# A wait for landing behind every group of four gathers on GpSimd

## The reference

```
q = (h @ Wq.T + bq)[dst];  k = (h @ Wk.T + bk)[src];  v = (h @ Wv.T + bv)[src]
alpha = sum(q * k, -1) / 4
ex = exp(alpha - segment_max(alpha, dst)[dst])
out = segment_sum(ex / segment_sum(ex, dst)[dst] * v, dst)
```

```
msg = silu([x[src], x[dst], rbf(length)] @ mw1 + mb1) @ mw2 + mb2
agg = segment_sum(msg, dst) / count
```

## Times and profile before

| | us |
|---|---|
| median of three timed runs | 5630.9 |
| the profiled execution, its span | 7840.1 |
| PE busy in it | 4625.7 (59%) |
| DVE busy | 4037.4 (51%) |
| POOL busy | 3849.3 (49%) |
| ACT busy | 2769.9 (35%) |
| share of the DMA engines' time, queue of the gathers | 23.6% |

### The profile page before, as it was taken

The page is one execution under the profiler, slowest core; times in us unless marked ns, Lnnn a source line. Parts: engine busy times, 40 slices in busy tenths (PEclk is TensorE's granted clock), DMA queues, the critical chain, the costliest instruction groups (busy, mean ns, idle before and its releaser), DMA issues.

```text
span 7840.1 us, 106032 instructions
## 1 busy us (share of the span) xinstructions
PE 4625.7 (59%) x22831; PEld 3727.9 (48%) x22832; DVE 4037.4 (51%) x11107; ACT 2769.9 (35%) x6493; POOL 3849.3 (49%) x4066
## 2 busy tenths in 40 slices
PE   4555555655556556555555565555555656666667
PEld 2444444534444445344444453444444545555555
DVE  4555555645555556455555565555555553333334
ACT  1333333423333334233333342333333432323333
POOL 3555555335555553345555543455555425555553
PEclk6666666676666666766666667666666677877887
DMA  5222222222322222222223222222322211111111
GB/s 127 78 79 76 77 76 78 52 66 73 79 78 77 78 80 56 69 67 79 76 78 79 78 62 69 68 78 77 80 78 79 60 33 43 44 44 44 44 44 30
DMA packets 267188, 536.13 MB, mean 68 GB/s; under 512 B 116253, under 2 KB 148689, under 8 KB 266509
## 3 DMA queue, kind: packets, MB, share of 16 engines
q0 software_dynamic: 180992, 490.24, 23.6%
q1 hardware_dynamic: 78901, 35.89, 1.9%
q10 hardware_dynamic: 6936, 6.69, 0.3%
HBM read 512.41 MB, written 18.03 MB: 68 GB/s over the span
## 4 chain that ended last, share of the span: by engine, by line
PE 26%; another core or an unknown queue 26%; issue 20%; DVE 17%; ACT 5%; DVEq 4%; ACTq 1%; SPq 0%; DMA 0%; POOL 0%; POOLq 0%
PE bank L806 9%; PE bank L825 7%; DVE acc L1265 6%; ACT oh L556 2%; DVEq L333 2%; PE bank L797 2%; PE bank L851 2%; PE bank L810 1%; DVE alpha L1288 1%; PE bank L879 1%; DVEq L1265 1%; DVE slots L1361 1%; DVE oh L1249 1%; PE bank L1001 1%
## 5 line engine op out<-in xcount | busy, mean ns | idle before, releaser
L508 POOL DMA_INDIRECT slots<-kv_table,idx x3224 | 3065.2, 951 | 3133.0 <-PE bank L825 1275.8
L825 PE MATMUL bank<-slots,oh 128*128 128x136 f32 (+1 forms) x8060 | 1593.0, 351 | 569.1 <-DVE acc L1265 506.4
L806 PE MATMUL bank<-qs,ohT 128*128 x8080 | 1685.7, 356 | 235.1 <-ACT ohT L547 129.2
L825 PEld LDWEIGHTS bank<-slots,oh 128*128 128x128 f32 x8060 | 1411.7, 252 | 704.7 <-DVE acc L1265 608.2
L806 PEld LDWEIGHTS bank<-qs,ohT 128*128 128x128 f32 x8080 | 1434.4, 257 | 456.6 <-issue 434.4
L1265 DVE TENSOR_TENSOR acc<-acc,bank 128x136 f32 (+1 forms) x4030 | 1172.0, 291 | 614.6 <-PE bank L825 171.5
L1282 DVE TENSOR_TENSOR slots<-slots,bank 128x512 f32<-128x512 f32 x808 | 551.8, 683 | 1322.6 <-remote 1291.5
L547 ACT ACTIVATE ohT<-bank,miss 128x512 f32<-128x512 f32 x1010 | 676.7, 683 | 1367.9 <-PE bank L797 1234.5
L508 POOL DMA_INDIRECT slots<-src_table,idx x806 | 760.4, 943 | 756.9 <-DMA idx<-src_e 247.9
L843 PE MATMUL bank<-ident,alpha 128*128 128x128 f32 x204 | 93.7, 459 | 1487.2 <-DVE alpha L1288 1481.7
L556 ACT ACTIVATE oh<-iota,rel_e 128x128 f32<-128x128 f32 x3168 | 962.8, 387 | 0.0
(11 more groups left out here) (257 smaller groups left out, 4079.5 us busy)
## 6 DMA issues: line engine op xcount, KB each, us to landing
slots<-kv_table,idx POOLq DMA_INDIRECT x3224
kv_table<-slots SPq DMA_DIRECT2D x20, 660.0 KB, 3.4
slots<-src_table,idx POOLq DMA_INDIRECT x806
resets<-flat_len ACTq DMA_DIRECT2D x51, 128.0 KB
idx<-src_e SPq DMA_DIRECT2D x255, 8.0 KB
terms<-flat_rel SPq DMA_DIRECT2D x255, 12.0 KB
resets<-flat_rst SPq DMA_DIRECT2D x2, 1551.0 KB
w<-in_w SPq DMA_DIRECT2D x8, 256.0 KB
```

What stands on the lines that cost most here:

```text
L508: pool.indirect_dma_start(slots[:, k, t, 0:width], None, table, bass.IndirectOffsetOnAxis(ap=idx[:, k, t:t + 1], axis=0))\
L806: mm = pe.matmul(o, ohT[:, j % 2, t, :], qs[:, blocks[j * G + t], 0:HID], start=True, stop=basis is None)
L825: mm = pe.matmul(bank[6 + part % 2][:, o:o + width], oh[:, k % 2, t, :], slots[:, k, t, HID:HID + width], start=True, stop=True)
```

## The change

`gather_chunk` gets the round `i` as an argument more, and behind the four gathers of each group (two groups in the last chunk) GpSimd waits until `kv_in[k][j]` has the number that `landed(l, i, k, j)` gives for this group.

```
             def gather_chunk(k, turn, l, i, table, width, places=CH):
...
                         pool.indirect_dma_start(slots[:, k, t, 0:width], None, table,
                                                 bass.IndirectOffsetOnAxis(ap=idx[:, k, t:t + 1], axis=0))\
                             .then_inc(kv_in[k][j], 16)
+                    pool.wait_ge(kv_in[k][j], landed(l, i, k, j))
...
-                        gather_chunk(k, turn_of(l, i, k), l, kv_table, KVW)
+                        gather_chunk(k, turn_of(l, i, k), l, i, kv_table, KVW)
...
-                    gather_chunk(k, turn_of(l, FULL, k), l, table, width, min(CH, PLACES - (RING * FULL + k) * CH))
+                    gather_chunk(k, turn_of(l, FULL, k), l, FULL, table, width, min(CH, PLACES - (RING * FULL + k) * CH))
...
-                    gather_chunk(k, turn_of(L, i, k), L, src_table, HID)
+                    gather_chunk(k, turn_of(L, i, k), L, i, src_table, HID)
```

More of the change, by code:

```diff
@@ L490, in _ @@
                     pool.reg_mov(uses[k][j], 0)
-            def gather_chunk(k, turn, l, table, width, places=CH):
+            def gather_chunk(k, turn, l, i, table, width, places=CH):
                 groups = -(-places // G)
```

## The result

The changed kernel takes 8086.4 us (median of 4 runs, 8080.1 to 8089.6) against 5630.8 us before: the ratio is 1.436 [1.434, 1.438]. 7850 us were forecast, in a range from 6200 to 8200.

What follows compares the result with a forecast made beforehand. The prediction took GpSimd's gathers as the bound, with the consumers within a few per cent; 1010 groups of 7.2 us (7272) plus 585 us around them gave 7857, forecast as 7850 us, range 6200 to 8200.

Steps and rivals of the forecast that it cites:

- 585 around it: Time beside the gathers: 53.3 us at the start, 435.6 between stages, 45.7 at the end, five tails of some 10.
- the consumers' stage: Attention stage by the consumers' pace: 103.5 us to the first multiply plus 50 x 18.85, 1046 us, about GpSimd's 1007.5.
- The lead of 3.6 chunks: GpSimd's head start at a stage's beginning, used up by about the tenth chunk, so hiding nothing of the stage's end.
- The price of a wait: Behind each group of four gathers: landing plus restart, 2.5 us (1.6 to 2.67), making a group 7.2 us instead of 5.0.
- the sign of being right: In every stage's trace, gathers come in fours with 2.0 to 2.7 us between them, released by a landing.
- The bound of 2.54 us for the landing: Longest time from a gather's start to its rows' arrival, up to 1.6 us beyond GpSimd's bar.
- The sum: Whole kernel: 1010 groups of 7.2 us, 7272 us, plus 585 us beside them, giving 7857 us.
- the multiplies run just behind the landings: DVE's multiplies, from about a stage's tenth chunk: chunks of 28.8 us are 10 us over the consumers' 18.85.
- The sum against the profiled execution's own time: Cross-check from the 7840.1 us span: stages grow from 7041 to 7272 us, tails shrink by 217, giving 7854 us.
- A: GpSimd's waits cost less in timed runs because tracing slows its pitch or the landing: 6040 to 7300 us; chance 0.16.
- B: GpSimd already pauses between bursts, so only the difference is paid: 5870 us, 6020 at the upper end; chance 0.10.
- C: Pauses after each four gathers let TensorE's signals through sooner: not slower, about 40 us less, 5590 us; chance 0.05.

Runs made afterwards that it cites:

- first profile: Kernel before, unchanged, the profile the prediction was read from: one execution spanning 7840.1 us, against a timed median of 5630.9 us.
- second profile: Kernel before, unchanged, profiled again in a follow-up: measured 5619.3 us, ratio 1.0001, with a span that fits the timed runs.

## Why the prediction was right

**That the long profile was not what is timed, and that GpSimd is the bound.** Right. The sum of 1.25 us times 4030 and 585 around it gave 5622 us from the first profile's rows; the second profile has stages of 1012.1, 1008.9, 1009.2, 1008.9 and 1006.2 us, 5045 together, and 573 around them. GpSimd's pitch within a burst was the same in both profiles, so it could be read from the disturbed one.

**That the consumers' stage would be as long, 1046 us.** Wrong, without a consequence for the forecast (it cost the 5660 us expected of one wait a round). Its 103.5 us from the first gather to the first multiply were the first profile's; in the second profile the second layer's first multiply starts 27.6 us behind its first gather. With 50 x 18.85 that is 970 us, under GpSimd's 1009, and the run with one wait a round showed that nothing hides a wait. The lead of 3.6 chunks that the prediction gave GpSimd at a stage's start came from the same 103.5 us: in the kernel after it is one chunk, 28.8 us in the second layer from first gather to first multiply. The conclusion, that the lead hides nothing, is the same.

**The price of a wait.** The step is right and its size a little low. 2.5 us were taken, with 1.6 and 2.67 as ends; the trace has 2.73 on average over all stages. For k and v that is 2.66 within a chunk, about the upper end, and 2.9 to 3.3 in front of a chunk's first gather, outside the 2.0 to 2.7 that were named as the sign of being right; in the message stage it is 2.38 within a chunk (medians). The page of the kernel after splits it: a gather is in place 2.8 us (median) from its issue, 1.85 behind its bar of 0.949, so some 0.8 us go into the restart. The bound of 2.54 us for the landing, read from the silence of the DMA engines, was too low: behind the gather of 1007.93 in the kernel after, their share is 0.00 from 1010.47 us on, and the multiply that waits for the landing starts at 1010.86. By the Trainium skill's page DMA: Bandwidth & Descriptors, section "Anatomy of one DMA — SWDGE (gpsimd) path", the two gathers would take 2.31 and 2.15 us (estimates from its fit); the trace has 2.8 and 2.5, and its numbers decide.

**The sum.** Forecast: 1010 x 7.2 = 7272 in the stages and 585 around them. Measured: 1539.3 + 1515.5 + 1518.1 + 1513.5 + 1444.9 = 7531 from first to last gathers, and 547 around them. Of the 259 us more in the stages, some 110 are the pauses in front of a chunk's first gather, which were not counted apart (3.0 us on average with k and v, 50 in each of four layers, 2.7 in the message stage, against the 2.5 taken). Some 120 are the pauses within a chunk, 2.66 us on average; about 24 of them are the first layer's, with the late landings beside the `resets` loads (13.8 us is the longest wait above). The rest is small gaps within groups, less what the rounding to 7.2 and the one wait too many in each stage had added. That the rest came out 38 us under the 585 has mainly one reason: the last multiply starts 3.5 us behind a stage's last gather, not 10.

**That the multiplies run just behind the landings.** Right: DVE's 2209.4 us before the landing.

**The sum against the profiled execution's own time**, 7854 against 8078.3, has the same stages of 7272 us in it and so says no more than the first sum. That it lies within 0.2% of the 7840.1 us of the first profile is chance and means nothing: the stages of that execution were stretched by stops that the kernel doesn't have.

**The rivals.** A (cheaper in the timed run) falls with the pitch of 1.25 in a profile that is as long as the timed runs. B (most of the pauses are there already) and C (a pause lets TensorE through) both rested on the stops of the first profile; the second profile has none, so there is no pause to share and nothing to let through. C's bound on the pitch, "below 0.9 us", also leaves out the fourth gather's own bar: 4.75 - 2.04 - 0.946 us leave 0.59 for each of three pitches, which speaks against C even more. What made DVE and GpSimd wait for "remote" in the first profile stays open; no run here repeated it.

**Two readings that were off and changed nothing.** Of the eight gathers that GpSimd is said to issue during DVE's stop of 8.11 us, five start within it. And the index loads were not ahead in the first profile: GpSimd waited for them 48 times there, 271.7 us. In the kernel after it waits for them once, 23.8 us, at the start.

## What to carry to other kernels

GpSimd issues these gathers back to back and is the bound, so each wait for the newest one cost the rest of its landing and the restart: 2.4 to 3 us a wait in every run where it waited for its newest group with k and v, added up one by one over 60 to 1010 waits. A wait for the group before the newest one cost nothing here, except beside the large loads at the start. Where a profile's span is far from the timed runs, take from it only what is the same everywhere in it, such as a pitch, and set up the sum so that it gives the time before.

## What the runs showed of the hardware beyond what was expected

One indirect gather of 128 rows on GpSimd has one pitch in all five stages of the kernel before: bars of 0.946 us and 0.30 us between them, whether it brings 135,168 or 65,536 bytes; the bytes show in the landing, 2.8 against 2.5 us in the kernel after.

Landings were late by several us while large loads were under way: pauses of 8.29 and 11.71 us for the group before the newest, beside two loads of 1551 KB. That the loads are the cause was not tested apart.
